# Transposing more tiles by DMA and reordering the end of attention in a fused attention, layer norm and routed-FFN kernel

## The chip, the cores and the metric

One Trainium2 chip, a single launch on 8 of its cores. The sequence of 8192 rows is cut into 8 stretches of 1024 rows, one for each core; the cores exchange nothing. The time is that of the slowest core, in microseconds (us) on the device.

## The reference, cut to what matters

```
x = layernorm(x + attention(x))
x = layernorm(x + ffn(x))

attention: 32 heads of 64, blocks of 512 queries, each against its own and the previous block,
           masked to a distance below 512, an additive bias that depends on the distance alone,
           a sink in the maximum and in the denominator; the heads joined, times Wo (2048 x 2048)
ffn:       x @ weight.T (2048 x 2048) + 2 * sum over the 2 best of 8 experts of
           w_e * (x @ A_e.T) @ B_e.T, rank 16; the w_e are the two best softmax values, rescaled
```

x is [8192, 2048] float32. The kernel computes its matrix products in bfloat16 with float32 sums.

## The kernel before, in words

A core holds its 1024 rows and the 512 before them as three blocks of x, transposed, in bfloat16 (XT[0] to XT[2]). Attention runs over 16 pairs of heads. A pair has 8 steps u (two blocks n of four query tiles c), u = 8 pr + 4 n + c, and the main loop (from line 812) takes two steps in each turn, so a pair is four turns: pair 13 is u = 104 to 111, pair 14 is 112 to 119, pair 15 is 120 to 127.

In a turn TensorE computes the scores of both steps for both heads hh (line 447) into the six PSUM banks psS. VectorE adds the bias and takes the row's minimum (462), ScalarE takes the exponent (492), VectorE takes the reciprocal and scales (500, 504). The 128x640 result has to be transposed, five 128x128 blocks, before the product with V (pv, 542). There are two ways for it. Either TensorE transposes the blocks into the bank psT (516) and VectorE, or for odd tiles of pair 15 ScalarE, copies them out (532, 530); or SP issues one DMA transpose (510). by_dma (476) says which: head 1 goes by DMA for u from 4 to 119, head 0 for odd tiles with u from 8 to 103, all else goes by TensorE. The order on every engine is the order in which the program puts instructions on that engine's queue.

Between these steps stand "units", groups of 16 matmuls of 512 columns (or 32 of 256) that fill one bank: the K, Q and V projections of this and the next pair (379, 392, 410). window_work queues them, and a turn takes two of them: one in bank 1 or 3 (begun after the scores, cut into shares around the transposes), one in bank psP. When a pair's product with V is due is kept in pending_pv: two turns after its scores where head 1 goes by DMA, one turn after where it does not.

Pair 15 has no next pair. Its units are pieces of the product with Wo: EARLY, four groups (t, oc) of output tile t and column block oc, with 15 of their 16 matmuls; after pv of pair 15, block 0, the four groups LATER, the last matmuls of EARLY, and the other groups for t = 0 to 3. held_adds keeps the additions of finished groups into the residual R1[t] (588, VectorE) until the end of the turn; such an addition waits for the load of R1[t] (r_tok). After the loop two more units run, then pv of pair 15, block 1, then the remaining units (feed.drain), and then 16 groups of Wo for tiles t = 4 to 7.

norm1 is the first layer norm of a tile (613). Its result y is cast to bfloat16 (620, ScalarE) and transposed: y_transpose puts 8 transposes of 128x128 on TensorE (627) and a 128x1024 copy out of psT on ScalarE (631), two such halves for a tile, between the groups of Wo (tiles 0 to 3) and between those of the FFN (tiles 4 to 7). Two buffers YB hold the casts. The router (644) of a tile and its FFN groups (681, 689) read the transposed y, which takes the place of the attention output in AT. The second layer norm and the stores (719) end the kernel.

Loads: GpSimd issues all weight loads (198) and those of R1[0] to R1[3] (743) from one queue, in program order, each behind its waits; weights are cast from float32 on the way. Wo's four column blocks lie in WO0 and in XT[0], XT[1], XT[2], so that blocks 1 to 3 can be loaded only when x is no longer needed. The loads come in this order: R1[0] and Wo block 0 in pair 13; R1[1] in the third turn of pair 14; R1[2], Wo 1 and Wo 2 at its last turn; R1[3] and Wo 3 in pair 15. R1[0] lies where WV[0] was. SP issues the bias tables (327), the DMA transposes, the loads of R1[4] to R1[7] and the stores.

Of the kernel before, what the change touches and what calls it, by code (L numbers as in the profile page):

```python
# [10 lines left out]
ACT = mybir.ActivationFunctionType  # L11
# [6 lines left out]
NI = 16  # L18
# [14 lines left out]
class Plan:  # L33
# [9 lines left out]
    def put(self, eng, fn, after=(), mark=False, dma=False):  # L43
        after = [t for t in after if t is not None]
        signal = None
        if dma:
            ring = DMA_RING[eng]
            sem = ring[self.turn[eng] % len(ring)]
            self.turn[eng] += 1
            if self.value[sem]:  # L50
                after.append((sem, self.value[sem]))
            self.value[sem] += 16
            signal = (sem, 16)
        elif mark:
            sem = ENGINE_SEM[eng]
            self.value[sem] += 1
            signal = (sem, 1)
        waits = []
        for s, v in after:
            if eng == "T" and s == "sT":  # L60
                continue
            if self.waited[eng].get(s, 0) < v:
                self.waited[eng][s] = v
                waits.append((s, v))
        self.queue[eng].append((fn, waits, signal))
        return (signal[0], self.value[signal[0]]) if signal else None
# [45 lines left out]
def build_program(nc):  # L112
# [55 lines left out]
    WT = [LATE1 + 16384, WO0, XT[0], XT[1]]  # L168
    ART = LATE1 + 16384 + 8192
    BTT = ART + 2176  # L170
    YB = [BTT + 2048, BTT + 4096]
    SCX = [YB[1] + 2048 + 128 * k for k in range(4)]
    SCT = [SCX[3] + 128 + 128 * k for k in range(8)]
    RTS = [SCT[7] + 128 + 128 * k for k in range(2)]
    assert LATE0 + 16384 <= LATE1 and RTS[1] + 128 <= LATE2
# [294 lines left out]

    def pslot(u, hh):
        if hh == 0 and by_dma(u, 0):
            return WO0 + 656 * (u // 2 % 3)
        return PB[hh][u % PBN[hh]]

    def by_dma(u, hh):
        if hh == 0:
            return steps[u][2] % 2 == 1 and 8 <= u < 104
        return 4 <= u < 120

    slot_user = {}

# [41 lines left out]
    def unload(u, hh):  # L524
        pr, n, c = steps[u]
        dst = b(PT[n][hh] + c * 640, [1, 640])
        src = p(psT, 0, [1, 640])
        after = [tr_tok[u, hh], pv_last.get((pr - 1, n))]
        if pr == 15 and c % 2:
            tok = put("S", lambda s: s.activation(dst, src, ACT.Copy), after=after, mark=True)  # L530
        else:
            tok = put("V", lambda v: v.tensor_copy(dst, src), after=after, mark=True)  # L532
        pt_tok[u, hh] = psT_free[0] = tok

    def pv(pr, n):
# [69 lines left out]
        return put("S", lambda s: s.activation(f(ls + 64, [1, 1]), f(ls + 66, [1, 1]), ACT.Exp,  # L605
                                               scale=-0.5), after=[l], mark=True)

    yb_tok, yb_free = {}, {0: None, 1: None}

    def norm1(t):  # L610
        ls = LNS[t]
        rs = ln_scales(t)
        ln_tok[t] = r_tok[t] = put("V", lambda v: v.tensor_scalar(
            f(R1[t], [1, DM]), f(R1[t], [1, DM]), f(ls + 60, [1, 1]), f(ls + 64, [1, 1]),
            ALU.subtract, ALU.mult), after=[rs, stat_tok[t]], mark=True)
        if t in (4, 5):
            y_cast(t)

    def y_cast(t):
        yb_tok[t] = put("S", lambda s: s.activation(b(YB[t % 2], [1, DM]), f(R1[t], [1, DM]),  # L620
                                                    ACT.Copy),
                        after=[ln_tok[t], yb_free[t % 2], late_tok[0]], mark=True)
    yt_tok = {}

    def y_transpose(t, half):
        for k in range(8):
            tok = put("T", lambda e, k=k: e.transpose(
                p(psT, k * 128, [1, 128]), b(YB[t % 2] + (half * 8 + k) * 128, [1, 128]),
                b(IDB, [1, 128])), after=[yb_tok[t], psT_free[0], t_id], mark=(k == 7))
        yb_free[t % 2] = tok  # L630
        yt_tok[t] = psT_free[0] = put("S", lambda s: s.activation(
            b(AT + half * 8 * 1024 + t * 128, [1024, 8], [1, 128]),
            p(psT, 0, [128, 8], [1, 128]), ACT.Copy), after=[tok], mark=True)
        if half == 1 and t + 2 in ln_tok:
            y_cast(t + 2)

    scx_tok, scx_free = {}, dict.fromkeys(range(4))
    sct_tok = {}
# [128 lines left out]
    feed.add(lambda k: in_turn(q_group(0, 0, 5), k_group(0, 1, 6), k_group(1, 1, 0)))  # L767
    feed.drain()

    EARLY = [(0, 0), (1, 0), (2, 0), (0, 1)]  # L770
    LATER = [(3, 0), (1, 1), (2, 1), (3, 1)]

    def window_work(pr):
        if pr == 0:
# [20 lines left out]
    def pv_due(m):  # L795
        if pending_pv and m >= pending_pv[0][0]:
            _, pr, n = pending_pv.popleft()
            pv(pr, n)
            if pr == 15 and n == 0:
                for t, oc in LATER:  # L800
                    wo_unit(t, oc)
                for t, oc in EARLY:
                    wo_unit(t, oc, NI - 1, NI)
                for oc in (2, 3):
                    for t in range(4):
                        wo_unit(t, oc)
            return True
# [4 lines left out]
    for u in range(0, U + 1, 2):  # L812
        pr, n, c = steps[u]
        m = u // 2
        if n == 1 and c == 0:
            if pr + 2 < NPAIR:
                load_wk(pr + 2)
                load_wq(pr + 2)
            if pr == 14:
                load_r(1, "G", [wk_done[14], wq_done[14]])  # L820
            if pr == 15:
                load_r(3, "G", [wk_done[15], wq_done[15]])
                load_wo(3, [wk_done[15], wq_done[15], wv_done[7]])
        scores(u)
        for w in (u, u + 1):
            for hh in range(2):
# [5 lines left out]
        if n == 0 and c == 2 and pr % 2 == 1:  # L832
            if pr // 2 + 2 < 8:
                load_wv(pr // 2 + 2)
            if pr == 13:
                load_r(0, "G", [wv_done[6]])
                load_wo(0, [tr_tok[v, 0] for v in (99, 101, 103)], width=512)
        if n == 1 and c == 2:
            if pr + 1 < NPAIR:
# [22 lines left out]
        feed.run()  # L862
        if n == 1 and c == 2 and pr + 2 < NPAIR:
            load_bias(pr + 2)
        if pr == 14 and n == 1 and c == 2:
            load_r(2, "G", [wv_done[7]])
            load_wo(1, [wk_done[15], wv_done[7]])
            load_wo(2, [wq_done[15], wv_done[7]])
        for add in held_adds:
            add_chunk(*add)  # L870
        held_adds.clear()
# [6 lines left out]
    held_adds = None  # L878

    feed.run()  # L880
    for _ in range(2):
        feed.begin()
        feed.run()
    pv_due(m + 1)
    U += 1
    late = [pv_last[15], at_tok[15, 1], e_tok[U, 0], e_tok[U, 1]]
    for t in range(4, 8):
# [6 lines left out]
        t_rep[k] = vop(lambda v, k=k: v.memset(f(RTS[k] + 32, [1, 8]), HUGE), *late)  # L894
    feed.drain()

    y_cast(0)
    y_cast(1)
    idx = 0
    for oc in range(4):  # L900
        for t in range(4, 8):
            for w in wo_group(t, oc):
                pass
            idx += 1
            if 3 <= idx < 11:
                y_transpose((idx - 3) // 2, (idx - 3) % 2)
        if oc < 3:
            wt_tok[oc + 1] = load_cast(WT[oc + 1], wt_in, (oc + 1) * 128, NI * 512, 8192,
                                       after=[wo_done[oc]])
# [12 lines left out]
    held.append((1, 1) + ffn_main(1, 1))  # L922
    for h in held[2:]:
        ffn_low(*h)
    y_transpose(4, 0)
    rest = [(t, oc) for oc in range(1, 4) for t in range(4)][2:]
    for idx, (t, oc) in enumerate(rest):
        ffn_low(t, oc, *ffn_main(t, oc))
        if idx < 7:
            y_transpose(4 + (idx + 1) // 2, (idx + 1) % 2)  # L930
        if idx in (1, 3, 5, 7):
            router(4 + idx // 2)
        if idx >= 8:
            scx_transpose(idx - 4)
# [75 lines left out]
```

How the kernel before makes its waits and increments, by code:

```python
            def run(eng):  # L70
                for fn, waits, signal in items:
                    for s, v in waits:
                        eng.wait_ge(sems[s], v)
                    ins = fn(eng)
                    if signal is not None:
                        ins.then_inc(sems[signal[0]], signal[1])
# [870 lines left out]
    def finish_all(y):  # L947
        ins = None
        for s in DMA_RING["Y"]:
            if plan.value[s]:
                ins = y.wait_ge(sems[s], plan.value[s])
        return ins
```

## Time and profile before

| what | value |
|---|---|
| median of 3 runs | 875.3 us (873.71 to 965.73) |
| the profiled execution | 878.33 us |
| its span on the slowest core (core 2) | 876.8 us |
| spans of the other cores | 868.7 to 871.9 us |
| mean granted TensorE clock, core 2 | 0.981 |
| TensorE busy with matmuls | 814.2 us |
| VectorE, ScalarE busy | 492.1 us, 453.1 us |
| HBM read, written | 117.53 MB, 8.49 MB |

The span runs from the first to the last instruction on one core; the execution's own time is 1.5 us longer. Times within the trace are counted from the span's start. L447 is line 447 of the kernel. PE is TensorE's matmul, PEld its weight load, DVE is VectorE, ACT ScalarE, POOL GpSimd, SP SyncE. "[0.36 <-DVE sb L504]" behind a row of the timeline is idle time of the engine ahead of it and what ended that. For a DMA, the time to landing is from its issue to its arrival.

### The profile page before, as it was taken

The numbers are of one execution on the slowest core, as the hardware profiler recorded it, in microseconds if no ns is written. First come the engines' busy times: TensorE is split into PE (matmuls) and PEld (weight loads), VectorE is DVE, ScalarE is ACT, GpSimd is POOL, SyncE is SP. The second block draws the span as 40 slices with busy tenths as digits, with TensorE's granted clock in tenths as the row PEclk, the third lists the DMA queues.
The fourth block names the chain that finished last, engine by engine and source line by source line (L and its number), as shares of the span: only waits on it lengthen the run. The fifth ranks groups of instructions, "written<-read, shape, count | busy, mean of one in ns | idle before, by whom it ended". The sixth has DMA issues, their size and how long they took to land.

```text
span 876.8 us, 17337 instructions; the slowest of 8 cores (868.7 to 876.8 us)
## 1 busy us (share of the span) xinstructions
PE 814.2 (93%) x5556; PEld 462.1 (53%) x5637; DVE 492.1 (56%) x1276; ACT 453.1 (52%) x993; POOL 123.9 (14%) x233
## 2 busy tenths in 40 slices
PE   3599999979999999999999999998799999998995
PEld 1345565656656647656556566563344445454443
DVE  2026666646666666666666666656565436546443
ACT  2145676746767667676777676765400512134101
POOL 7001302302122031030130114002000000000000
PEclk9889999999999999999999999999799999999998
DMA  9999999797697697797898869739939465003212
GB/s 125 161 168 146 90 137 140 84 141 112 86 173 115 88 158 93 129 151 97 129 114 130 139 130 175 118 74 166 191 84 220 106 121 97 1 1 145 96 49 96
DMA packets 150857, 104.72 MB, mean 119 GB/s; under 512 B 115024, under 2 KB 138576, under 8 KB 149232
## 3 DMA queue, kind: packets, MB, share of 16 engines
q0 software_dynamic: 32544, 53.52, 41.0%
q1 hardware_dynamic: 118224, 50.08, 33.0%
q8 instruction: 47, 0.77, 0.4%
q14 instruction: 42, 0.34, 0.2%
HBM read 117.53 MB, written 8.49 MB: 144 GB/s over the span
## 4 chain that ended last, share of the span: by engine, by line
PE 80%; DMA 6%; DVE 4%; issue 4%; ACT 3%; POOL 1%; SPq 1%; DVEq 0%; ACTq 0%; POOLq 0%
PE psS L379 11%; PE psS L681 10%; PE psS L410 9%; PE psP L410 8%; PE psS L562 8%; PE psP L392 8%; PE psP L379 6%; PE psS L447 5%; PE psT L542 4%; DMA sb<-xt 4%; PE psT L516 4%; PE psS L392 3%; PE psP L562 2%; DMA sb<-sb 2%; ACT sb L492 1%
## 5 line engine op out<-in xcount | busy, mean ns | idle before, releaser
L462 DVE CUSTOM_DVE_ANT_0 sb<-psS,sb 128x640 f32<-128x640 f32 x256 | 218.7, 882 | 170.5 <-PE psS L447 141.4
L492 ACT ACTIVATE sb<-sb 128x641 bf16<-128x641 f32 x256 | 212.3, 830 | 114.9 <-DVE sb L462 107.5
L379 PE MATMUL psS<-sb 128*128 128x512 bf16 x480 | 115.6, 383 | 3.0 <-DMA sb<-wk 1.5
L681 PE MATMUL psS<-sb 128*128 128x512 bf16 (+1 forms) x437 | 98.3, 375 | 0.6
L504 DVE TENSOR_SCALAR sb<-sb 128x640 bf16<-128x640 bf16 x256 | 88.8, 388 | 14.1 <-DVE sb L500 0.5
L410 PE MATMUL psP<-sb 128*128 128x256 bf16 x736 | 86.9, 273 | 0.1
L562 PE MATMUL psS<-sb 128*128 128x512 bf16 x376 | 86.4, 379 | 0.5
L410 PE MATMUL psS<-sb 128*128 128x256 bf16 x736 | 85.4, 273 | 0.0
L392 PE MATMUL psP<-sb 128*128 128x512 bf16 x347 | 81.1, 379 | 2.1 <-issue 1.4
L338 ACT ACTIVATE sb<-sb 128x512 f32<-128x512 f32 (+2 forms) x192 | 76.2, 470 | 6.4 <-DMA sb<-gscr 6.4
L379 PE MATMUL psP<-sb 128*128 128x512 bf16 x257 | 64.7, 387 | 15.2 <-DMA sb<-xt 14.7
L588 DVE TENSOR_TENSOR sb<-psS,sb 128x512 f32<-128x512 f32 (+1 forms) x56 | 38.2, 683 | 70.3 <-PE psS L689 32.8
L410 PEld LDWEIGHTS psS<-sb 128*128 128x128 bf16 x736 | 71.6, 98 | 11.5
L410 PEld LDWEIGHTS psP<-sb 128*128 128x128 bf16 x736 | 69.7, 98 | 14.2 <-issue 6.5
L379 PEld LDWEIGHTS psS<-sb 128*128 128x128 bf16 x496 | 47.7, 99 | 52.7 <-issue 4.7
L532 DVE COPY sb<-psT 128x640 bf16<-128x640 bf16 x84 | 41.1, 489 | 52.4 <-PE psT L516 52.4
L681 PEld LDWEIGHTS psS<-sb 128*128 128x128 bf16 x448 | 43.2, 98 | 48.2
L198 POOL DMA_DIRECT2D sb<-wk x58 | 31.3, 570 | 223.4 <-PE psS L379 166.7
L562 PEld LDWEIGHTS psS<-sb 128*128 128x128 bf16 x386 | 37.0, 98 | 41.6
L392 PEld LDWEIGHTS psP<-sb 128*128 128x128 bf16 x368 | 34.0, 98 | 43.6 <-issue 6.1
L602 ACT ACTIVATE sb<-sb 128x1 f32<-128x1 f32 x16 | 4.7, 292 | 101.1 <-DVE sb L600 101.1
L516 PE MATMUL psT<-sb 128*128 128x128 bf16 x460 | 41.0, 220 | 11.5 <-DVE sb L504 8.8
(111 smaller groups left out, 816.8 us busy)
## 6 DMA issues: line engine op xcount, KB each, us to landing
sb<-gscr SPq DMA_DIRECT2D x32, 320.0 KB, 9.4
sb<-wt POOLq DMA_DIRECT2D x4, 2048.0 KB, 14.8
sb<-wv POOLq DMA_DIRECT2D x56, 128.0 KB, 7.8
sb<-wk POOLq DMA_DIRECT2D x56, 128.0 KB, 9.9
sb<-wq POOLq DMA_DIRECT2D x56, 128.0 KB, 10.1
y<-sb SPq DMA_DIRECT2D x14, 512.0 KB, 3.3
sb<-xt POOLq DMA_DIRECT2D x12, 512.0 KB, 39.7
sb<-wo POOLq DMA_DIRECT2D x12, 512.0 KB, 23.1
```

Of the source, the lines that this page charges most:

```text
L338: tok = put("S", lambda e, dst=dst, src=src, fn=fn, bias=bias: e.activation(dst, src, fn, bias=bias), after=after + [bias_tok[pr, hh], t_f ...
L379: tok = put("T", lambda t, i=i: t.matmul(bank_ap(bank, [1, 512]), b(WK[pr % 2] + i * 128, [1, 128]), b(XT[blk] + i * 512, [1, 512]), start ...
L392: tok = put("T", lambda t, i=i: t.matmul(bank_ap(bank, [1, 512]), b(WQ[pr % 2] + i * 128, [1, 128]), b(XT[blk + 1] + i * 512, [1, 512]), s ...
L410: tok = put("T", lambda t, i=i, half=half, blk=blk, part=part: t.matmul(p(tens, off + 256 * half, [1, 256]), b(XT[blk] + i * 512 + part * ...
L447: tok = put("T", lambda t, hh=hh, base=base, c0=c0, w=w, tile=tile: t.matmul(p(psS[hh], base + c0, [1, w]), b(QT[pr % 2] + tile * 128, [1, ...
L462: tok = put("V", lambda v: v.tensor_tensor_reduce(out=f(SX[hh], [1, 640]), in0=p(psS[hh], T1 if c % 2 else T0, [1, 640]), in1=f(table, [1, ...
L492: e_tok[u, hh] = put("S", lambda s: s.activation(b(pslot(u, hh), [1, 641]), f(SX[hh], [1, 641]), ACT.Exp, bias=f(st + 4 * hh + 2, [1, 1]), ...
L504: norm_tok[u, hh] = put("V", lambda v, hh=hh, pb=pb: v.tensor_scalar_mul(b(pb, [1, 640]), b(pb, [1, 640]), f(st + 12 + 2 * hh, [1, 1])), a ...
L516: tr_tok[u, hh] = put("T", lambda t, k=k: t.transpose(p(psT, k * 128, [1, 128]), b(pslot(u, hh) + k * 128, [1, 128]), b(IDB, [1, 128])), a ...
L532: tok = put("V", lambda v: v.tensor_copy(dst, src), after=after, mark=True)
L562: return put("T", lambda e: e.matmul(bank_ap(bank, [1, 512]), b(AT + i * 1024 + t * 128, [1, 128]), b(WO[oc] + i * 512, [1, 512]), start=f ...
L681: put("T", lambda e, i=i: e.matmul(bank_ap(bank, [1, w]), b(AT + i * 1024 + t * 128, [1, 128]), b(WT[oc] + i * 512 + c0, [1, w]), start=(i ...
```

## The change

- by_dma takes head 0's odd tiles up to u = 119 and head 1 to the end. Head 0's DMA tiles of u from 104 on use three buffers in WV[0] in place of those in WO0. Pair 15's remaining TensorE transposes (head 0) are all copied out by VectorE.
- y of every tile is transposed by one DMA of 128x2048 from SP (y_turn), four buffers YB in place of two; y_transpose is gone.
- EARLY has six groups, LATER two; after the loop, units run until six are left, and then pv of pair 15, block 1.
- Wo 1 is loaded a turn earlier (third turn of pair 14), R1[0] later (first turn of pair 15, after the transposes of steps 115, 117 and 119, since their buffers lie where it goes), and R1[3] and Wo 3 are put behind it there.

```diff
-    YB = [BTT + 2048, BTT + 4096]
+    YB = [BTT + 2048 + 2048 * k for k in range(4)]
...
         if hh == 0 and by_dma(u, 0):
-            return WO0 + 656 * (u // 2 % 3)
+            return (WO0 if u < 104 else WV[0]) + 656 * (u // 2 % 3)
...
         if hh == 0:
-            return steps[u][2] % 2 == 1 and 8 <= u < 104
-        return 4 <= u < 120
+            return steps[u][2] % 2 == 1 and 8 <= u < 120
+        return u >= 4
...
-        if pr == 15 and c % 2:
-            tok = put("S", lambda s: s.activation(dst, src, ACT.Copy), after=after, mark=True)
-        else:
-            tok = put("V", lambda v: v.tensor_copy(dst, src), after=after, mark=True)
+        tok = put("V", lambda v: v.tensor_copy(dst, src), after=after, mark=True)
...
+    def y_turn(t):
+        cast = put("S", lambda s: s.activation(b(YB[t % 4], [1, DM]), f(R1[t], [1, DM]), ACT.Copy),
+                   after=[ln_tok[t], yb_free.get(t % 4), late_tok[0]], mark=True)
+        yt_tok[t] = yb_free[t % 4] = put("Y", lambda y: y.dma_start_transpose(
+            out=b(AT + t * 128, [1024, NI], [1, 128]), in_=b(YB[t % 4], [1, DM])),
+            after=[cast], dma=True)
...
-    EARLY = [(0, 0), (1, 0), (2, 0), (0, 1)]
-    LATER = [(3, 0), (1, 1), (2, 1), (3, 1)]
+    EARLY = [(1, 0), (1, 1), (2, 0), (2, 1), (0, 0), (0, 1)]
+    LATER = [(3, 0), (3, 1)]
...
             if pr == 15 and n == 0:
+                for t, oc in EARLY:
+                    wo_unit(t, oc, NI - 1, NI)
                 for t, oc in LATER:
                     wo_unit(t, oc)
-                for t, oc in EARLY:
-                    wo_unit(t, oc, NI - 1, NI)
...
-            if pr == 15:
-                load_r(3, "G", [wk_done[15], wq_done[15]])
-                load_wo(3, [wk_done[15], wq_done[15], wv_done[7]])
...
             if pr == 13:
-                load_r(0, "G", [wv_done[6]])
                 load_wo(0, [tr_tok[v, 0] for v in (99, 101, 103)], width=512)
...
+        if pr == 14 and n == 1 and c == 0:
+            load_wo(1, [wk_done[15], wv_done[7]])
         if pr == 14 and n == 1 and c == 2:
             load_r(2, "G", [wv_done[7]])
-            load_wo(1, [wk_done[15], wv_done[7]])
-            load_wo(2, [wq_done[15], wv_done[7]])
+            load_wo(2, [wk_done[15], wq_done[15], wv_done[7]])
+        if pr == 15 and n == 0 and c == 0:
+            load_r(0, "G", [wv_done[6]] + [tr_tok[v, 0] for v in (115, 117, 119)])
+            load_r(3, "G", [wk_done[15], wq_done[15]])
+            load_wo(3, [wk_done[15], wq_done[15], wv_done[7]])
...
-    for _ in range(2):
+    while len(feed.work) > 6:
         feed.begin()
         feed.run()
-    pv_due(m + 1)
+    pv_due(m + 2)
...
-    y_cast(0)
-    y_cast(1)
-    idx = 0
+    for t in range(4):
+        y_turn(t)
     for oc in range(4):
         for t in range(4, 8):
             for w in wo_group(t, oc):
                 pass
-            idx += 1
-            if 3 <= idx < 11:
-                y_transpose((idx - 3) // 2, (idx - 3) % 2)
```

norm1 calls y_turn(t) for t above 3, and the eight places in the FFN part where y_transpose stood are empty.

## Rows read from the trace of the kernel before

**Rows 1.** The page: busy time of the engines, TensorE's clock in 40 slices.

```profile
PE 814.2 (93%) x5556; PEld 462.1 (53%) x5637; DVE 492.1 (56%) x1276; ACT 453.1 (52%) x993; POOL 123.9 (14%) x233
...
PEclk9889999999999999999999999999799999999998
```

**Rows 2.** Stretches: us, busy PE, PEld, DVE, ACT, POOL; PEclk, DMA share, GB/s.

```profile
482.70:517.09 34.39, 33.98 (x259) 20.71 (x261) 22.09 (x60) 24.24 (x56) 4.39 (x8) 1.00 0.69 125
517.09:554.08 36.99, 36.07 (x283) 21.64 (x282) 23.81 (x64) 24.57 (x56) 12.82 (x24) 1.00 1.15 158
554.08:591.05 36.97, 35.79 (x280) 21.59 (x280) 23.80 (x64) 24.56 (x56) 1.71 (x4) 1.00 0.47 92
591.05:602.07 11.02, 9.52 (x64) 4.44 (x62) 6.67 (x17) 7.33 (x18) 6.49 (x12) 1.00 1.05 182
...
614.38:628.26 13.88, 8.60 (x62) 4.67 (x60) 6.54 (x17) 5.63 (x11) 0.00 (x0) 0.75 1.03 210
628.26:647.81 19.55, 18.64 (x109) 8.66 (x110) 11.00 (x24) 5.47 (x11) 0.00 (x0) 0.92 0.30 61
...
797.55:867.35 69.80, 67.37 (x338) 32.60 (x343) 33.48 (x66) 12.65 (x25) 0.00 (x0) 1.00 0.27 106
```

**Rows 3.** TensorE's timeline, last turn of pair 14 (start, duration, line, count, idle before).

```profile
581.64 0.72 PE L447 MATMUL psS<-sb 64*128 64x384 bf16 x8
...
586.86 0.44 PE L516 MATMUL psT<-sb 128*128 128x128 bf16 x5 [0.26 <-DVE sb L504]
...
588.61 0.44 PE L516 MATMUL psT<-sb 128*128 128x128 bf16 x5
...
589.85 1.28 PE L542 MATMUL psT<-sb 128*64 128x512 bf16 x16
```

**Rows 4.** TensorE's timeline, third turn of pair 15.

```profile
614.38 0.72 PE L447 MATMUL psS<-sb 64*128 64x384 bf16 x8
...
619.78 0.44 PE L516 MATMUL psT<-sb 128*128 128x128 bf16 x5 [1.34 <-DVE sb L504]
...
625.99 2.34 PE L542 MATMUL psT<-sb 128*64 128x512 bf16 x16 [0.94 <-ACT sb L530]
```

**Rows 5.** TensorE's timeline, y's transposes in the Wo stage, router of tile 7.

```profile
686.46 0.61 PE L627 MATMUL psT<-sb 128*128 128x128 bf16 x8
686.90 3.62 PE L562 MATMUL psS<-sb 128*128 128x512 bf16 x15
690.36 0.61 PE L627 MATMUL psT<-sb 128*128 128x128 bf16 x8
...
798.85 1.11 PE L644 MATMUL psS<-sb 128*128 128x136 bf16 x16 [1.29 <-ACT sb L631]
```

**Rows 6.** Line 198, Wo 1's first load: its issue, time to landing.

```profile
L198 POOL DMA_DIRECT2D sb<-wo x1: 527/527/527, 590.5 to 590.5; - x1
...
DMA to landing us min/median/max: 8.2/8.2/8.2
```

**Rows 7.** Line 743, load of R1[3], behind Wo 1 and Wo 2.

```profile
L743 POOL DMA_DIRECT2D sb<-xr x1: 652/652/652, 596.0 to 596.0; - x1
...
DMA to landing us min/median/max: 28.5/28.5/28.5
```

**Rows 8.** Line 198, pair 15's Q weights, last of pair 13's loads.

```profile
L198 POOL DMA_DIRECT2D sb<-wq x4: 567/580/596, 534.6 to 536.1; - x4
...
DMA to landing us min/median/max: 12.1/12.4/14.6
```

**Rows 9.** DMA queues, 568 to 574 us: two DMA transposes, nothing else (share of 6 us).

```profile
q1 hardware_dynamic: 1344, 0.33, 28.5%
...
sb<-sb SPq DMA_TRANSPOSE x2, 2.6
```

**Rows 10.** Line 510, DMA transposes issued under Wo 0's load, time to landing.

```profile
L510 SPq DMA_TRANSPOSE sb<-sb x3: 1201/1340/1608, 524.8 to 533.5; - x3
...
DMA to landing us min/median/max: 9.9/10.5/12.9
```

More of the change, by code:

```diff
@@ L170, in build_program @@
     BTT = ART + 2176
-    YB = [BTT + 2048, BTT + 4096]
-    SCX = [YB[1] + 2048 + 128 * k for k in range(4)]
+    YB = [BTT + 2048 + 2048 * k for k in range(4)]
+    SCX = [YB[3] + 2048 + 128 * k for k in range(4)]
     SCT = [SCX[3] + 128 + 128 * k for k in range(8)]
@@ L606, in ln_scales @@
                                                scale=-0.5), after=[l], mark=True)
-    yb_tok, yb_free = {}, {0: None, 1: None}
+    yb_free, yt_tok = {}, {}
     def norm1(t):
@@ L615, in norm1 @@
             ALU.subtract, ALU.mult), after=[rs, stat_tok[t]], mark=True)
[L616 to L635, printed above, removed]
+        if t > 3:
+            y_turn(t)
[5 more added lines that the diff above has]
+            after=[cast], dma=True)
     scx_tok, scx_free = {}, dict.fromkeys(range(4))
@@ L895, in build_program @@
     feed.drain()
-    y_cast(0)
-    y_cast(1)
-    idx = 0
+    for t in range(4):
+        y_turn(t)
     for oc in range(4):
@@ L924, in build_program @@
         ffn_low(*h)
-    y_transpose(4, 0)
     rest = [(t, oc) for oc in range(1, 4) for t in range(4)][2:]
@@ L928, in build_program @@
         ffn_low(t, oc, *ffn_main(t, oc))
-        if idx < 7:
-            y_transpose(4 + (idx + 1) // 2, (idx + 1) % 2)
         if idx in (1, 3, 5, 7):
```

## The prediction

> **What bounds the kernel now.** I read the page first [rows 1]: TensorE is busy 93% of the span and its clock is granted in full but for the start and one slice near 70% of the span. VectorE and ScalarE are busy about half the time. So what counts is the length of TensorE's own queue and its gaps. Busy time by stretch [rows 2] says where the gaps are. Pair 12 (482.70 to 517.09) takes 34.39 us with 33.98 busy. Pairs 13 and 14 do the same eight units and take 36.99 and 36.97. Pair 15 has the real hole: its third turn (614.38 to 628.26) takes 13.88 us for 8.60 of busy time, part of it at a clock of 0.75, and the clock is still at 0.92 in the stretch behind it. Behind pair 15 TensorE is busy almost without a break to the end, the last 69.80 us with 67.37. A TensorE instruction that is dropped behind pair 15 is therefore worth its whole start-to-start time; in pair 15 it is latency and order that count.
>
> All sums are made against the profiled execution, 878.3 us (span 876.8 and 1.5 around it). The median of the runs is 875.3, 3.0 below; I subtract the gain from the median.
>
> **A. y by DMA.** TensorE loses 16 blocks of 8 transposes. One block takes from 686.46 to the next matmul at 686.90, 0.44 us [rows 5]: 16 x 0.44 = 7.0. Router 7 also waited 1.29 us for ScalarE's copy [rows 5], which goes too. Together 8.3 us, and ScalarE loses 16 copies of psT, which bound nothing. What is late next is the DMA. For tiles 0 to 3 the casts follow the last norm, and the routers that need them stand behind 16 groups of Wo: 16 x 16 matmuls at 3.46 us (686.90 to 690.36; one record of the sixteen is missing) [rows 5] = 55 us. A DMA transpose of five blocks holds all 16 DMA engines for 28.5% of 6 us / 2 = 0.85 us and lands in 2.6 us [rows 9]; one of sixteen blocks is 3.2 times that, 2.7 us of DMA and 8.3 to landing. Four in a row are 33 us at the most when nothing else runs, under 55. Under a heavy load the landing was 9.9 to 12.9 for five blocks [rows 10], but that is mostly waiting, which four transposes in flight share. For tiles 4 to 7, router 4 stands eight groups behind the last Wo group, 28 us, and the later ones further. I take no wait: cost 0, the bounds being 0 and the case of the rivals below. The FFN loads of weights start earlier with the matmuls that release them and are not late.
>
> **B. Pairs 13 and 14 like the others.** Head 0's odd tiles leave TensorE: 4 x 0.28 us a pair, and the wait for the scaled exponent ahead of a first transpose (0.26 in the turn shown [rows 3]) no longer meets a second one. What remains is pair 12's program, so I take its time: (36.99 + 36.97) - 2 x 34.39 = 5.2 us. Bounds: 2.2 (the transposes alone, 8 x 0.28) and 5.2. The risk is DMA. Pair 13 has a DMA share of 1.15 [rows 2], and its transposes land up to 12.9 us after issue [rows 10]; four more add 4 x 0.85 = 3.4 us of DMA work. The product with V of pair 13, block 0, comes at about 550, some 17 us behind the issue of the last of its transposes (533.5 [rows 10]), so some 2 to 4 us are left. I take the upper end.
>
> **C. Pair 15.** The common structure of a turn is that of pair 14 [rows 3]: the first transpose can start 5.2 to 5.7 us behind the scores (581.64 to 586.86), the second at 7.0 (588.61). Of TensorE's queue the scores take 0.65 and a product with V 1.21 (0.72 and 1.28 with the tail of the last instruction [rows 3]), a set of five transposes 0.28 (0.44 with its tail; five of the eight of rows 5), a matmul 0.216 (3.46 / 16 [rows 5]). Today each turn has four such sets with copies on two engines between them, so that in the third the product with V starts 11.6 us behind the scores (614.38 to 625.99) [rows 4]. With two sets:
> - turn 1: scores 0.65, 16 matmuls of Q, 6 of the first group, wait 0.3, set, 9 matmuls, set, 3 of the next: 8.85
> - turn 2: first set at 5.4, second at 7.0, the rest of the group, product with V of pair 14: 9.2
> - turn 3: 8.55
> - turn 4: 12 matmuls are left behind the scores, then the six begun groups are used up and the hole comes here: sets at 5.4 and 7.1, VectorE's copy, product with V at 8.0, end at 9.2.
> That is 35.8. Then 6 + 64 matmuls = 15.1 cover the last DMA transposes (under 13 us by rows 10), and the product 1.2: 52.1 us from 591.05's counterpart to the end of attention, against 56.8 today (591.05 to 647.81, [rows 2]). In it are 176 matmuls of 512 columns, today 141; the 35 more are no longer done behind it: 35 x 0.216 = 7.6. Gain before costs 56.8 - 52.1 + 7.6 = 12.3.
>
> First cost: the clock. Now the hole ends with the clock at half: the product with V takes 2.34 [rows 4] in place of 1.28 [rows 3], and with the scores and matmuls behind it the fall costs some 2.9 us, inside the 56.8. The new hole in turn 4 is about 4.7 us with 0.6 busy; I expect the same fall, 2.5 us. Bounds 0 and 3.4 (6.8 us at half speed, the length of that stretch).
>
> Second cost: R1[0]. Its load moves from pair 13 to behind Wo 1, R1[2] and Wo 2 in one queue, and its first addition is that of the fifth begun group, in VectorE's queue at the end of turn 3, ahead of all of turn 4. With B's gain Wo 1 is issued at about 576.3 (turn start 568.7, value group done 7.6 later), turn 4 starts at 612.4. Bound below: today's bulk stretch, where Wo 1's first piece took 8.2 us [rows 6] and R1[3], issued at 596.0, landed at 624.5 [rows 7], is 3.03 to 3.3 us for each MB read; 10 MB from 576.3 with some 5 us to start end at 611 to 612, no delay. Bound above: pair 13's stretch, 6 MB from the first issue of Wo 0 at about 522 to 536.1 + 14.6 = 550.7 [rows 8] with DMA transposes and bias tables between, 4.7 us a MB: 623.3, 11 us late. The first rate is that of the same loads in the same sizes, but without transposes; seven of those at 0.85 us [rows 9] make up to 6 us, part of which fits into gaps. I take landing at 615, a delay of 3 us, because the price lies nearer to the first row.
>
> Wo 1 itself has landed at about 594 where its last rows are first read at 597; Wo 2 and Wo 3 are needed at 630 and 645 and are in by 618 and 632. Those I cost at nothing. The other cores share these gaps in the same way.
>
> C is 12.3 - 2.5 - 3 = 6.8. Sum: 8.3 + 5.2 + 6.8 = 20.3, so 858.0 for the profiled execution and **855.0** against the median.
>
> **A rule that speaks against it.** The rows show five blocks in 2.6 us alone, one engine-time of 0.17 us a block [rows 9]. The Trainium skill, "VectorE: DVE Perf Modes", section "The three transpose paths", gives 390 ns for a 128x128 bf16 transpose on TensorE and 1309 ns by DMA, and its rules for authors prefer TensorE where PSUM is a possible destination. By its figure a tile of 16 blocks would be 20.9 us and the four first ones 84, an estimate from that page. On time alone inside a DMA of five blocks the trace does not agree: five times its figure is 6.5 us where 2.6 were measured. What is saved here is TensorE's 0.055 us a block (0.44 / 8).
>
> **Rivals.**
> 1. *R1[0] is in time.* No delay, sum 23.3: 852.0; if the clock holds as well, 849.5. For it: the bulk rate of rows 6 and 7. Against it: those loads ran without transposes. Chance 0.25.
> 2. *The loads take back the pair 15 gain.* At the rate of rows 8 R1[0] is 11 us late, C is 12.3 - 2.5 - 11 = -1, sum 12.3: 863.0. VectorE stands at that addition with all bias steps of turn 4 behind it. For it: pair 13's stretch is just such a mixture. Against it: pair 15 has no bias tables and fewer small loads. Chance 0.22.
> 3. *The DMA mixture slows pairs 13 and 14* (a product with V waits on a late transpose), B is nothing and R1[0] is late as forecast: 860.2. For it: a share above 1 in pair 13. Chance 0.07.
> 4. *Slower: y's transposes are the new wait.* If one of 16 blocks takes as long for each block as the five under load (12.9 / 5 = 2.6 us a block [rows 10], 41 us) and they follow one another, the four take 165 us against the 50 that the Wo groups leave, and TensorE stands before the routers for over 100. It decides from 12.5 us a tile; from about 17.5 a tile (4 x 17.5 = 70, wait 20) the whole gain is gone, and at 20 a tile the result is 885. For it: the landing times under load, and the four fall beside R1 loads of 4 MB and a block of FFN weights. Against it: 0.85 us of DMA for five blocks. Chance 0.05. By the rule of the Trainium skill named above, 20.9 us a tile, this is the case that comes.
>
> **How the numbers follow.** The forecast (delay 1 to 6 us, 851.5 to 857.5) has 0.41, the rivals 0.25, 0.22, 0.07, 0.05. Two per cent, 857.8, is about what a measurement of this kernel can tell from no change. Below it lie rival 1 and nine tenths of the forecast, 0.61; rivals 2 and 3 and the rest are within it, 0.34; slower 0.05. The range 847 to 866 reaches from rival 1 with its clock full and 2 to spare to rival 2 with a delay a few us longer, and leaves rival 4 out.
>
> **What would show it.** Pairs 13 and 14 at 34.4 us each. No transposes of y on TensorE and no idle time ahead of the routers. In pair 15, turns of about 9 us and TensorE idle 4 us or more in the last, with VectorE's addition of tile 0 released by the DMA of xr about 3 us late, and the clock at half once behind it. Attention's end at about 643 (585.9 + 52.1 + 5.5), against 647.8, with the 35 matmuls done. The forecast is wrong if routers wait for SP's transposes, if a product with V waits for a DMA in pairs 13 to 15, if TensorE waits for Wo, or if the wait for xr is 0 or above 8 us.

## The result and the profile after

The changed kernel is slower: 937.4, 944.4, 956.4 and 967.9 us in four runs. The ratio is 1.076, 95% interval 1.058 to 1.094; it sets the two faster of these against the undisturbed runs of the kernel before, and the two slower ones lie further off still. Forecast were 855.0 us and, at most, 866. The profiled execution took 937.36 us.

The first thing to read is the view of the cores. Before, the eight spans lay between 868.7 and 876.8 us. Now they differ by up to 65 us, though all cores run the same program:

```profile
core 0: 886.0 us, clock 0.970
core 1: 935.8 us, clock 0.946
...
core 6: 871.0 us, clock 0.981
```

The page of core 1, to be set beside [rows 1]: TensorE's busy time is the same (813.3 us against 814.2), its share of the span fell from 93% to 87%, and the chain of waits now has 14% of DMA and 11% of SP's queue in it.

```profile
PE 813.3 (87%) x5429; PEld 454.8 (49%) x5429; DVE 489.9 (52%) x1270; ACT 431.0 (46%) x969; POOL 123.0 (13%) x233
...
PE 65%; DMA 14%; SPq 11%; DVE 3%; issue 3%; ACT 2%; POOL 1%; DVEq 0%; ACTq 0%; POOLq 0%
```

TensorE's waits behind attention on core 1 (total, times, longest), and its timeline there. Line 630 is the router, and what it waits for, sb<-sb, is the DMA transpose of y:

```profile
PE psS L630 <- DMA sb<-sb: 59.7, 2, 32.6
...
PE psP L630 <- DMA sb<-sb: 1.2, 1, 1.2
```

```profile
730.64 1.11 PE L630 MATMUL psS<-sb 128*128 128x136 bf16 x16
764.38 1.97 PE L630 MATMUL psS<-sb 128*128 128x136 bf16 x16 [32.64 <-DMA sb<-sb]
793.40 1.97 PE L630 MATMUL psS<-sb 128*128 128x136 bf16 x16 [27.04 <-DMA sb<-sb]
```

Router 0 starts at once, router 1 stands for 32.6 us and router 2 for 27.0. So rival 4 has come, the one that was given 0.05. The longest wait of that kind on the other cores, 0 and 2 to 7, was 18.4, 32.9, 25.4, 16.2, 41.5, 0 (core 6) and 37.2 us.

Now DMA. Line 619 is the issue of y's transpose by SP (durations of the issue, then the time to landing); first core 1, then core 6:

```profile
L619 SPq DMA_TRANSPOSE sb<-sb x8: 1957/3188/59051, 681.5 to 800.5; - x8
...
DMA to landing us min/median/max: 4.5/7.9/101.3
```

```profile
L619 SPq DMA_TRANSPOSE sb<-sb x8: 1766/4758/13752, 681.5 to 738.7; - x8
...
DMA to landing us min/median/max: 4.5/9.1/19.8
```

One issue held SP for 59 us and its transpose landed after 101. The loads of the FFN weights beside them suffered as much: the last three took 54.5, 80.9 and 77.0 us on core 1, against 13.9 to 15.9 on core 6 and 14.0 to 15.2 in the kernel before. This is the DMA view of 680 to 800 us in 40 slices of 3 us, GB/s and the weight loads' median time to landing, core 1 and then core 6:

```profile
GB/s 284 310 291 224 140 22 39 53 98 67 106 120 114 148 135 173 134 113 125 108 101 69 50 34 21 20 13 14 37 20 14 151 33 52 36 24 37 25 240 225
...
sb<-wt POOLq DMA_DIRECT2D x3, 2048.0 KB, 77.0
```

```profile
GB/s 290 306 299 220 122 177 161 195 166 267 177 263 182 250 183 246 175 189 212 144 176 0 3 0 0 0 0 0 5 0 0 0 0 0 0 5 0 295 218 188
...
sb<-wt POOLq DMA_DIRECT2D x3, 2048.0 KB, 15.3
```

On core 6 everything is over at 743 us. On core 1 the DMA engines are busy by their records (share 1.3 in 745 to 764 us) and move 13 to 50 GB/s. I call that a jam. In the packet records of the trace a row of a weight load is one packet of 16 KB and takes 1.23 us; a transpose's packets are 256 bytes and take 0.018 us when alone; on core 1 between 750 and 760 us they take 0.99 us in the mean.

Attention has a stall of its own, on every core (4.6 to 9.4 us). Core 6, pair 15's second turn, to be set beside [rows 4], and GpSimd's queue there:

```profile
602.05 0.81 PE L559 MATMUL psS<-sb 128*128 128x512 bf16 x3
610.40 2.34 PE L539 MATMUL psT<-sb 128*64 128x512 bf16 x16 [7.54 <-DMA sb<-sb]
612.67 1.25 PE L447 MATMUL psS<-sb 64*128 64x384 bf16 x8
```

```profile
610.19 1.10 POOL L729 DMA_DIRECT2D sb<-xr  x2 [23.03 <-DMA sb<-sb]
```

The product with V of pair 14's second block waits 7.5 us for the DMA transposes of steps 118 and 119, after which the clock is at half (2.34 us for what takes 1.28). They had been issued at 582 to 587 us beside the loads of Wo 1 and 2. The load of R1[0] waits for the same transposes and holds up GpSimd's queue for 23 us.

### The profile page after: what moved, and what is told of

Same layout as the page of the kernel before. It is cut to its first block, busy times and chain, and to the rows that moved or that the text cites. A ratio compares the mean times of both kernels' runs of the same rounds, so it can differ in the third digit from the quotient of the medians.

```text
span 935.8 us, 17019 instructions; the slowest of 8 cores (871.0 to 935.8 us)
## 1 busy us (share of the span) xinstructions
PE 813.3 (87%) x5429; PEld 454.8 (49%) x5429; DVE 489.9 (52%) x1270; ACT 431.0 (46%) x969; POOL 123.0 (13%) x233
## 4 chain that ended last, share of the span: by engine, by line
PE 65%; DMA 14%; SPq 11%; DVE 3%; issue 3%; ACT 2%; POOL 1%; DVEq 0%; ACTq 0%; POOLq 0%
DMA sb<-sb 10%; PE psS L379 10%; PE psS L667 9%; PE psS L410 8%; SPq L619 7%; PE psP L410 7%; PE psP L392 7%; PE psP L379 5%; PE psT L539 4%; DMA sb<-xt 4%; PE psS L447 4%; SPq L510 3%; PE psS L559 3%; PE psS L392 3%; PE psT L516 2%
## 5 line engine op out<-in xcount | busy, mean ns | idle before, releaser
L379 PE MATMUL psS<-sb 128*128 128x512 bf16 x496 | 118.7, 384 | 1.5 <-DMA sb<-wk 1.3
L559 PE MATMUL psS<-sb 128*128 128x512 bf16 x402 | 90.3, 383 | 0.0
L392 PE MATMUL psP<-sb 128*128 128x512 bf16 x368 | 83.7, 380 | 0.0
L379 PE MATMUL psP<-sb 128*128 128x512 bf16 x272 | 66.8, 387 | 14.8 <-DMA sb<-xt 14.8
L410 PEld LDWEIGHTS psS<-sb 128*128 128x128 bf16 x736 | 71.7, 98 | 11.6
L379 PEld LDWEIGHTS psS<-sb 128*128 128x128 bf16 x496 | 48.0, 99 | 54.1 <-issue 5.6
L667 PEld LDWEIGHTS psS<-sb 128*128 128x128 bf16 x448 | 43.7, 99 | 48.4 <-issue 1.3
L559 PEld LDWEIGHTS psS<-sb 128*128 128x128 bf16 x402 | 39.4, 99 | 47.6 <-issue 2.6
L529 DVE COPY sb<-psT 128x640 bf16<-128x640 bf16 x76 | 37.1, 488 | 47.4 <-PE psT L516 47.4
L630 PE MATMUL psS<-sb 128*128 128x136 bf16 x112 | 9.5, 249 | 59.7 <-DMA sb<-sb 59.7
## 6 DMA issues: line engine op xcount, KB each, us to landing
sb<-wq POOLq DMA_DIRECT2D x56, 128.0 KB, 10.4
```

Of the source, the lines that this page charges most:

```text
L379: tok = put("T", lambda t, i=i: t.matmul(bank_ap(bank, [1, 512]), b(WK[pr % 2] + i * 128, [1, 128]), b(XT[blk] + i * 512, [1, 512]), start ...
L392: tok = put("T", lambda t, i=i: t.matmul(bank_ap(bank, [1, 512]), b(WQ[pr % 2] + i * 128, [1, 128]), b(XT[blk + 1] + i * 512, [1, 512]), s ...
L410: tok = put("T", lambda t, i=i, half=half, blk=blk, part=part: t.matmul(p(tens, off + 256 * half, [1, 256]), b(XT[blk] + i * 512 + part * ...
L559: return put("T", lambda e: e.matmul(bank_ap(bank, [1, 512]), b(AT + i * 1024 + t * 128, [1, 128]), b(WO[oc] + i * 512, [1, 512]), start=f ...
L667: put("T", lambda e, i=i: e.matmul(bank_ap(bank, [1, w]), b(AT + i * 1024 + t * 128, [1, 128]), b(WT[oc] + i * 512 + c0, [1, w]), start=(i ...
```

## The experiments

Theory 1: a DMA transpose and a weight load in flight together jam, the more the longer the load's rows; everything that was lost was lost there. Rivals: the 16-block transpose is slow by itself; or pair 15 and the moved loads make the queues late. "Gated" below means y by DMA with two waits more.

### y by DMA alone

The kernel before with y_turn, four buffers YB and no y_transpose, as in the change's diff; nothing else.

> The kernel before with one edit: y of every tile by one DMA transpose. Theory 1 (convoy): a transpose's 256-byte packets take turns on each DMA engine with the packets of the FFN weight load, which are 16 KB and 1.2 us each, so the four y transposes of tiles 0 to 3 are held up as long as a weight load is in flight and hold it up in turn. Then this edit alone brings the routers' waits of 0 to 60 us, different from core to core, and 20 to 90 us on the slowest core's time: 890 to 960, with weight loads landing after 40 us and more on the cores that wait. Theory 2 (the pair 15 part and the moved loads make the queue late): no router waits here, and 875.3 - 8 = 867.

Measured: 904.2, 915.2 and 920.7 us. The cores:

```profile
core 0: 902.6 us, clock 0.967
core 1: 863.2 us, clock 0.987
core 2: 865.6 us, clock 0.985
core 3: 862.6 us, clock 0.989
```

Core by core seven are 2 to 11 us shorter than before; core 0 is not, with a router wait of 36.1 us and 16 to 68 GB/s in slices that add up to some 36 us. The slow-down is in this edit, and it is a matter of chance which core has it. In the last of the three runs six cores had it, by their spans (895 to 919 us against 865).

### The rest of the change alone

```diff
-        if t > 3:
-            y_turn(t)
+        if t in (4, 5):
+            y_cast(t)
```

and so on: y is back on TensorE.

> The changed kernel with y back on TensorE as before. Theory 1: no router waits and no spread between cores, the product with V in pair 15's second turn still waits 7.5 us for a DMA transpose, and attention with its 35 more matmuls ends near 653.5; against the kernel before that is a gain of 1 to 3 us, 872 to 875. Theory 2: here the slow-down shows, 900 or more.

Measured: 881.2 us, ratio 1.0067 (1.0047 to 1.0087). No large spread, as theory 1 has it; but it is 0.7% slower where 872 to 875 were expected. The wait at the second turn of pair 15 was 2.3 to 9.4 us by core.

### Narrower rows of the loads

FFN blocks by 16 DMAs of 512 columns; then Wo 1 to 3 too.

```diff
+    def load_wt(oc, after, width=512):
+        wt_tok[oc] = []
+        for j in range(0, 8192, width):
+            wt_tok[oc] += [load_cast(WT[oc] + j, wt_in, oc * 128, NI * 512, width, after=after,
                                      c0=j)] * (width // 512)
...
-    wt_tok[0] = load_cast(WT[0], wt_in, 0, NI * 512, 8192, after=late)
+    load_wt(0, late)
...
-    def load_wo(oc, after=(), width=2048):
+    def load_wo(oc, after=(), width=512):
```

> The changed kernel with each FFN weight block loaded by 16 DMAs of 512 columns (1 KB written a row) in place of one of 8192 columns (16 KB). Theory 1 (the neighbour's packet size sets the price): y transposes land in about 10 to 25 us, no router waits, all cores near core 6 of the changed kernel, 871 to 876. Rival (the transpose of 16 blocks is slow by itself or by its strided destination): waits as before, 900 or more.

> As the run before, and Wo's blocks 1 to 3 in pieces of 512 columns too. Theory 1: the wait of the product with V in pair 15's second turn (7.5 us, DMA transposes of steps 118 and 119 beside loads with 4 KB rows) goes with its half clock, 8 to 10 us less than the run before: 862 to 867. Rival (the transposes of pair 15 wait because the DMA engines are simply full, by bytes): that wait stays within 2 us, and the time with it.

Measured: 886.0 us, 1.0108 (1.0071 to 1.0145), and 882.6 us, 1.0067 (1.0043 to 1.0091). The jam is gone: on the four cores looked at in each run no slice of 4 us falls below 57 GB/s while both are in flight (in slices of 1.6 us it dips to 31). Some 50 to 85 us went with it. But neither reached the number. In the second a router waits 10 to 14 us on three cores, and on these three the median transpose of y lands after 18 to 19 us, on the other five after 10 to 14. That they take turns with sixteen times as many packets is the likely reason, but not shown. Core 2:

```profile
PE psP L630 <- DMA sb<-sb: 13.5, 1, 13.5
```

In attention the narrow pieces moved things the way that was expected. These are the landing times of the transposes issued from 584 us on (line 510, core 1), changed kernel, then narrow Wo:

```profile
DMA to landing us min/median/max: 23.1/25.0/26.8
```

```profile
DMA to landing us min/median/max: 17.0/18.0/19.1
```

The wait at the second turn fell from 4.6 to 9.4 us to 0 to 3.6. On core 5, where it is 0, the next turns show what it had hidden: the scores of the last turn wait 3.2 us for VectorE's addition of tile 0, whose R1[0] is late.

### Transposes and loads kept apart

```diff
+                                       after=[wo_done[oc], yt_tok[3]])
...
+    wt_tok[3] = load_cast(WT[3], wt_in, 3 * 128, NI * 512, 8192,
+                          after=[wo_done[2], yt_tok[7]])
```

The first line is for FFN blocks 1 and 2. Sizes are as they were.

> The kernel before with y by DMA, as in the run of that edit alone, and two waits more on GpSimd's queue: weight blocks 1 and 2 of the FFN are loaded only once the transposes of tiles 0 to 3 have landed, block 3 once that of tile 7 has. Transposes and loads are as large as before, they only don't overlap. Theory 1 (a jam between the two): transposes land in under 12 us, no router waits on any core, every core as the undisturbed ones of the ungated run (862 to 868), 866 to 869 for the whole, 1% faster than before. Rival A (the 16-block transpose is slow of itself): routers wait still. Rival B (the gated loads come too late): a wait of FFN matmuls for a weight load, 5 us or more.

> The changed kernel with those two waits and with Wo 1 to 3 in pieces of 512 columns. Theory 1: router waits gone, attention as in the run with narrow pieces; its undisturbed cores took 859 to 865, so 864 to 870 for the whole. If the pair 15 part is worth what was forecast of it, 4 us and more below the gated kernel with the old pair 15; if the wait for R1[0], the wait for tile (1,1)'s bank and the clock take it back, no difference of 2 us between the two.

Measured: 867.8 us, 0.9933 (0.9920 to 0.9946), and 868.2 us, 0.9949 (0.9931 to 0.9967). So with narrow Wo parts B and C together added nothing to the gain of A. Line 622 is the transpose's issue in the first, core 3, its slowest:

```profile
L622 SPq DMA_TRANSPOSE sb<-sb x8: 1362/2122/3267, 678.3 to 735.2; - x8
...
DMA to landing us min/median/max: 4.3/4.7/5.5
```

Eight transposes of 16 blocks, the same instructions as those that took up to 101 us, all land within 5.5 us, on each of the eight cores, and on none of them is a packet of an FFN block's load on record between the first and the last packet of the four transposes of a set. The rival "slow by itself" is out, and no load was late. What is left of the waits behind attention is one line, where the kernel before had 1.3 us on the same instruction (its line 670):

```profile
PE psT L659 <- ACT sb L663: 4.0, 2, 2.3
```

That is the transpose of the router's result. The transposes of y used to stand between it and the chain that it waits for.

### Shorter transposes; 1 KB and 4 KB rows; the changed kernel gated

All but the last are the kernel before with y by DMA, ungated.

```diff
+        for j in range(0, DM, 512):
+            yt_tok[t].append(put("Y", lambda y, j=j: y.dma_start_transpose(
+                out=b(AT + t * 128 + j // 128 * 1024, [1024, 512 // 128], [1, 128]),
+                in_=b(YB[t % 4] + j, [1, 512])), after=[cast], dma=True))
```

> The kernel before with y by DMA, each tile by four DMA transposes of four blocks in place of one of sixteen, weight loads as they were (rows of 16 KB). Theory 1: the packets are the same, 256 bytes beside 16 KB, so the jam comes as often: 890 or more on the slowest core, DMA rates of 15 to 60 GB/s for tens of us. Rival A (the long single transpose is what stalls): no router waits, 863 to 869.

> The kernel before with y by DMA, not gated, and the FFN weight blocks in 16 pieces of 512 columns. Theory 1: no jam (DMA rate not below 100 GB/s while both are in flight), but each transpose takes turns with more packets and lands in 10 to 20 us; the last of tiles 0 to 3 comes about when its router wants it, so waits of 0 to 15 us on some cores: 868 to 885. Rival (any overlap jams): 890 or more.

> The kernel before with y by DMA, ungated, the FFN weight blocks in four pieces with 4 KB written a row: between 16 KB rows (904 to 921) and 1 KB rows (868.2). If a jam needs packets much longer than the transposes' own, and grows with them, the DMA rate dips for some us on some cores and routers wait 0 to 10 us: 868 to 880. If any row above 1 KB jams as 16 KB does: 890 or more.

> The changed kernel with the two waits that keep the y transposes and the FFN weight loads apart, and nothing else. If their overlap is the whole of the slow-down, every core comes near core 6 of the changed kernel, the only one on which no router waited (871.0), and the time is 870 to 876, against 937 and more ungated. The 7.5 us wait at pair 15's second turn stays, Wo being wide. If something else of the change slows it too, 880 or more.

Measured: shorter transposes 885.1 us, 1.0108 (1.0073 to 1.0144), the longest router wait 18.0 us; 1 KB rows 868.2 us, 0.9938 (0.9921 to 0.9955); 4 KB rows 869.4 us, 0.9948 (0.9927 to 0.9968), no router wait; the changed kernel gated 875.5 us, 1.0010 (0.9995 to 1.0024). So four-block transposes beside 16 KB rows still cost 17 us but much less than 16-block ones, which was not expected: the length has a part in it. With rows of 4 KB or less in the FFN loads there was no jam. These edits change two things at once, since shorter rows also mean 4 or 16 smaller DMAs in place of one; which of the two ends the jam was not tested. And with the overlap taken out of the changed kernel its whole slow-down is gone, as is every gain. It differs from the gated kernel with narrow Wo (868.2) in the width of Wo's pieces alone, so wide pieces cost it some 7 us. Core 7 shows where, in the product with V of pair 15's second turn.

```profile
614.20 2.35 PE L539 MATMUL psT<-sb 128*64 128x512 bf16 x16 [10.19 <-DMA sb<-sb]
```

### Parts B and C one by one

R1[0] in halves, so that only columns that no begun group needs wait for head 0's buffers:

```diff
-            return (WO0 if u < 104 else WV[0]) + 656 * (u // 2 % 3)
+            return (WO0 if u < 104 else WV[0] + 2048) + 656 * (u // 2 % 3)
...
             if pr == 13:
+                load_r(0, "G", [wv_done[6]], 0, 1024)
...
-            load_r(0, "G", [wv_done[6]] + [tr_tok[v, 0] for v in (115, 117, 119)])
             load_r(3, "G", [wk_done[15], wq_done[15]])
             load_wo(3, [wk_done[15], wq_done[15], wv_done[7]])
+            load_r(0, "G", [tr_tok[v, 0] for v in (115, 117, 119)], 1024, DM)
```

> The gated changed kernel with narrow Wo pieces, and R1[0] loaded in two halves: columns 0 to 1023, which the two begun groups of tile 0 need, already in pair 13, the rest after Wo 3; head 0's three DMA buffers lie in the half that is loaded late. Theory R (R1[0] late costs some us, as forecast): the wait of the scores in pair 15's last turn for VectorE's addition (up to 3 us) goes, 2 to 4 us less than the kernel without this edit (868.2): 864 to 866. Rival (something else would be late at the same place, the clock stays at half): within 1.5 us of it.

Measured: 862.9 us, 0.9881 (0.9865 to 0.9898): 5.2 us less than without it (868.2, gated with narrow Wo). Not all of that is shown to be R1[0]'s lateness. The wait for its addition was 0.5 to 4.6 us by core before this edit and is gone on all eight. But GpSimd's queue is no longer held by transposes either, and on core 4 the wait ahead of the second turn's product with V fell too, so that the last turn already starts 4.7 us earlier; on other cores that wait fell or rose by up to 3 us. Core 4 before this edit, the second turn's product and the last turn of pair 15:

```profile
602.81 2.34 PE L539 MATMUL psT<-sb 128*64 128x512 bf16 x16 [4.30 <-DMA sb<-sb]
...
615.99 0.55 PE L447 MATMUL psS<-sb 64*128 64x384 bf16 x6
619.46 0.51 PE L447 MATMUL psS<-sb 64*128 64x384 bf16 x2 [2.91 <-DVE sb L585]
```

and with it, same core:

```profile
599.97 1.28 PE L539 MATMUL psT<-sb 128*64 128x512 bf16 x16 [1.49 <-DMA sb<-sb]
...
611.33 0.72 PE L447 MATMUL psS<-sb 64*128 64x384 bf16 x8
```

Part B alone (gated, pair 15 as before), wide and narrow Wo; part C alone (gated, narrow Wo, `8 <= u < 104`, R1[0] in pair 13):

> The kernel before with y by DMA gated, and of the rest only part B: head 0's odd tiles of pairs 13 and 14 by DMA, R1[0] in halves; pair 15, Wo's order and pieces as before. Forecast of part B: 5.2 us, so 862.6 against 867.8 of the gated kernel alone. Rival (the added transposes and the wide loads hold each other up): the product with V of pair 13 or of pair 14's second block waits 2 to 5 us and half of the gain or all of it is lost, 865 to 869.

> As the run before with Wo 1 to 3 in pieces of 512 columns. If the neighbour's packets set the price, the wait at pair 14's second block (in pair 15's second turn) is smaller here than there by 2 us and more; if the transposes of steps 118 and 119 land in time anyway, since pair 15's own are not in the queue, no difference beyond 1 us.

> The gated changed kernel with narrow Wo pieces, but without part B: head 0's tiles of pairs 13 and 14 on TensorE, R1[0] loaded in pair 13. Part C alone, then, against the gated kernel with the old pair 15 (867.8). Forecast of C without the wait for R1[0]: 12.3 - 2.5 = 10, 858. Rival (in pair 15 the first turns lose to waits for DMA transposes and bank additions what the begun groups gain): 866 or more, with 2 to 7 us of waits for DMA at the product with V.

Measured: B with wide Wo 870.7 us, 0.9974 (0.9953 to 0.9995), 2.9 us more than without B; with narrow Wo 866.4 us, 0.9925 (0.9901 to 0.9948), 1.5 less than without B, which its interval does not tell from nothing; C 863.2 us, 0.9883 (0.9866 to 0.9900), 4.7 less than the old pair 15. All three are set against the gated kernel with y by DMA (867.8), which has wide Wo; the same kernel with narrow Wo was not run, but in the wide one no product with V waits for a DMA on any core, so that narrow pieces had no such wait to take away. B with wide Wo, core 0, pair 15's second turn; the other seven cores have no wait there. At pair 13's product five cores wait 0.3 to 3.9 us, and three don't:

```profile
610.50 2.34 PE L542 MATMUL psT<-sb 128*64 128x512 bf16 x16 [8.48 <-DMA sb<-sb]
```

With narrow Wo none waits in the second turn, and the longest wait at pair 13's product is 1.8 us. Six of the eight cores of B with wide Wo took 857.8 to 861.1 us, those of the kernel without B 860.9 to 866.4: most cores gain, and the slowest, 868.8, is again a matter of chance. C alone, core 4, the starts of its turns and what breaks them:

```profile
585.51 0.72 PE L447 MATMUL psS<-sb 64*128 64x384 bf16 x8
...
604.01 0.72 PE L447 MATMUL psS<-sb 64*128 64x384 bf16 x8
...
613.41 0.81 PE L559 MATMUL psP<-sb 128*128 128x512 bf16 x3 [1.34 <-DVE sb L585]
614.15 0.72 PE L447 MATMUL psS<-sb 64*128 64x384 bf16 x8
...
623.24 2.34 PE L539 MATMUL psT<-sb 128*64 128x512 bf16 x16 [1.42 <-DVE sb L585]
626.53 0.58 PE L559 MATMUL psP<-sb 128*128 128x512 bf16 x1 [0.94 <-ACT sb L548]
...
643.65 1.28 PE L539 MATMUL psT<-sb 128*64 128x512 bf16 x16
```

From 585.51 to the end of the last product, 643.65 + 1.21, are 59.4 us, where the prediction had 52.1, or 54.6 with the clock. By its own sum that makes 56.8 - 59.4 + 7.6 = 5.0 us of gain, near the 4.7 measured.

## Why the prediction was wrong, point by point

**A, the step that failed.** "Under a heavy load the landing was 9.9 to 12.9 for five blocks [rows 10], but that is mostly waiting, which four transposes in flight share. [...] I take no wait: cost 0". The wait was not bounded by [rows 10], nor wholly shared: on core 1 routers 1 and 2 stood 32.6 and 27.0 us one after the other. Those rows were taken beside Wo 0, whose pieces have rows of 1 KB; the FFN blocks come in rows of 16 KB. I used a landing time without asking what stood beside it. The row on the FFN loads (2048 KB in one DMA) was on the page. Instead of 0, seven of the eight cores stood 16 to 61 us before their routers in the profiled run. Rival 4 named the place and the engine that stands, priced it by blocks, 2.6 us each, and set the chance by a transpose alone; the point from which it decides, 12.5 us a tile, fits the run with narrow rows, where cores with a median of 10 to 14 us a tile did not wait and those with 18 to 19 waited 10 to 14 us. Its price by blocks was not what came: the same transposes take 4.2 to 5.5 us each without those loads beside them.

**A, the gain.** With the overlap gone 5.7 us were gained, 873.6 to 867.8, where 8.3 were forecast. The 16 blocks went and router 7's wait too; 2.7 us came back at the transpose of the router's result (1.3 before, 4.0 after), for which the removed work was cover. The prediction has no term for this wait.

**The skill's figure.** 1309 ns a block by DMA (the Trainium skill, "VectorE: DVE Perf Modes", "The three transpose paths") does not fit: 16 blocks landed in 4.3 us when no FFN load ran beside them (the prediction had 8.3), 0.27 us a block. Its advice to prefer TensorE was right for this kernel as changed, for a reason that the page does not give, and wrong once the loads were kept away, where DMA was 5.7 us faster.

**B.** In TensorE's own queue the forecast held: on core 6 of the changed kernel pairs 13 and 14 take 69.4 us (515.87 to 585.29), 4.5 less than before (forecast 5.2). The cost fell one pair later. The product with V of pair 13, at which I looked for a wait, had 0 to 2.9 us of it by core; that of pair 14's second block, which I didn't look at, 4.6 to 9.4. Its transposes run beside Wo 1 and 2 with rows of 4 KB. But B by itself isn't enough for that stall: with B alone and wide Wo one core of eight had it, in the changed kernel all had, where pair 15's own DMA transposes and an earlier Wo 1 are added. Which of these two does it was not tested. With wide Wo B loses 2.9 us, with narrow Wo it gains 1.5, within the noise.

**C.** Forecast 12.3 less 2.5 for the clock; alone and with R1[0] in time it measured 4.7. Turns 1 and 2 came as forecast (9.0 and 9.5 us against 8.85 and 9.2). Turn 3 took 10.1 in place of 8.55: the sixth begun group takes the bank of the fourth, whose addition is held to the end of the turn, 1.34 us of wait, which the prediction has nowhere. Turn 4 took 12.4 in place of 9.2: the same additions stand ahead of the product with V (1.42), ScalarE's copy 0.94 behind it, and the clock at half, which came as forecast. The 70 matmuls took 17.1 in place of 15.1, part of them at half clock. The upper bound of the clock term, 3.4 us, was taken from 6.8 us at half clock, and that is short: by the granted clocks of [rows 2] the fall in the kernel before lasted 2 x (0.25 x 13.88 + 0.08 x 19.55) = 10 us.

**R1[0].** The mechanism was right: VectorE's addition of tile 0 waits for the load, and the scores of the last turn wait for it. Forecast were 3 us; the direct wait was 0.5 to 4.6 us by core in the gated kernel with narrow Wo. The edit that took it out gained 5.2 us, some of it elsewhere. In the changed kernel it does not show, because the 7.5 us wait ahead of it covers it: on core 6 R1[0] was issued at 610.2 and had landed by 619.4, before its addition at 622.6.

In the kernel with all three mends (gated, narrow Wo, R1[0] in halves) the three parts give 873.3 - 862.9 = 10.4 us; forecast were 20.3.

**What stays open.** Why the DMA engines, busy with one packet of 16 KB each, don't simply finish the load: eight rows for each engine are 10 us, yet loads took up to 81. That a transpose ties the engines to one another, so that each long packet on one stops all, would fit; no run shows it. Nor is it shown why a core jams in one run and not in the next, or why length matters for transposes of four against sixteen blocks. Whether row length or the number and size of the DMAs decides is open too. With narrow FFN rows the changed kernel took 886.0 us, but its profiled execution was the shortest of eight (873.6) and no router waits in it, so that what held the others wasn't seen. With narrow Wo as well (882.6) routers wait; in the kernel before with y by DMA and narrow FFN rows (868.2) they don't. This may come from y's transposes being issued 26 us behind the loads of R1[4] to R1[7] in the changed kernel (655.6 to 681.5, core 6) and 34 us in the other (643.0 to 676.8, core 5); that is argued, not tested.

## What to carry to other kernels

Before moving work to DMA, list what else is in flight at that time and how long the rows of it are; a landing time measured beside 1 KB rows says nothing about one beside 16 KB rows. Look at all cores: a cost that is a matter of chance hits the maximum over eight cores nearly always (here in all four runs of the changed kernel and all three of y by DMA alone), and a single core can look mended. And when work leaves a busy engine, ask which waits it stood in front of.

## What was not expected of the hardware

- A DMA transpose of 128x2048 landed in 4.2 to 5.5 us with no FFN load beside it and in up to 101 us beside a load with 16 KB rows; the load took up to 81 us in place of 14 to 16. Beside FFN loads with 4 KB rows the worst transpose on any core took 29.9 us and no router waited.
- While the two jam, the DMA share reads 1.3 and the rate is 13 to 50 GB/s; in the kernel before a share of 1.05 went with 182 GB/s [rows 2]. The share says nothing about progress, the rate does.
- One DMA issue can hold SP's queue for 59 us (72 on core 7), where it takes 1.3 to 3.3 us undisturbed.
